# All layers' rotary tables made in the first part, scores handed over by PSUM bank, and two VectorE pieces of the feed-forward moved

## The reference, cut to what matters

```python
xn = layernorm(x)                              # x: 2 x 1024 x 128
x = x + causal_attention(xn) + stack(xn)       # both read xn

# causal_attention: 16 heads of width 8, full 1024 x 1024 scores, softmax, then a
# scrambled transpose and @ W_O

# stack: 6 layers of
x = attn_layer(shift_tokens(x), ...) + x       # 16 heads of 64, windows of 32 + the one before
x = ffn_layer(shift_tokens(x), ...) + x
# attn_layer:
q = l2norm(q) * q_scale[i];  k = l2norm(k) * k_scale[i]
q = q * cos * scale + rotate_half(q) * sin * scale
k = k * cos / scale + rotate_half(k) * sin / scale
# ffn_layer: layernorm, gain, (a, gate) = xn @ W1 + b1, a * gelu(gate) @ W2 + b2
```

## Time and profile before

| | us |
|---|---|
| runs | 2111.00, 2115.48, 2120.15 (median 2115.48) |
| profiled execution, its own time | 2128.67 |
| span of the profiled execution | 2126.9 |
| busy: PE / DVE / POOL / ACT | 1940.5 / 1658.7 / 1418.3 / 1305.8 |
| mean granted clock of TensorE | 0.953 of full |

### The profile page before, as it was taken

The page is one execution under the profiler, slowest core; times in us unless marked ns, Lnnn a source line. Parts: engine busy times, 40 slices in busy tenths (PEclk is TensorE's granted clock), DMA queues, the critical chain, the costliest instruction groups (busy, mean ns, idle before and its releaser), DMA issues.

```text
span 2126.9 us, 74573 instructions
## 1 busy us (share of the span) xinstructions
PE 1940.5 (91%) x33032; PEld 1322.8 (62%) x33032; DVE 1658.7 (78%) x1635; ACT 1305.8 (61%) x1547; POOL 1418.3 (67%) x1403
## 2 busy tenths in 40 slices
PE   3989899589999999999899998899999999999985
PEld 1434444357767666776677776667767676676774
DVE  5765562489888888889888988887888888988862
ACT  1355457356667766667666765666776666766752
POOL 1000000699988898879888888597889887888820
PEclk7799999789999999999999999999999999999997
DMA  3141100033233333333223323233333333322221
GB/s 103 39 133 46 44 25 12 28 82 77 70 86 75 87 71 77 90 78 85 63 65 87 91 71 90 49 79 86 74 86 72 79 93 74 72 63 66 69 67 45
DMA packets 144033, 151.51 MB, mean 71 GB/s; under 512 B 60760, under 2 KB 85596, under 8 KB 142944
## 3 DMA queue, kind: packets, MB, share of 16 engines
q1 hardware_dynamic: 143712, 146.75, 27.5%
HBM read 35.75 MB, written 5.44 MB: 19 GB/s over the span
## 4 chain that ended last, share of the span: by engine, by line
PE 32%; DVE 22%; POOL 21%; issue 15%; SPq 5%; ACT 3%; DMA 1%; POOLq 0%; DVEq 0%; ACTq 0%
POOL arena L1109 8%; POOL arena L1117 5%; SPq L1273 4%; DVE arena L626 4%; PE banks L408 4%; DVE ss L713 3%; PE banks L471 3%; PE banks L538 3%; PE banks L480 3%; DVE mx_t L748 3%; PE banks L565 3%; PE banks L391 2%; PE banks L498 2%; DVE arena L721 2%; PE banks L511 2%
## 5 line engine op out<-in xcount | busy, mean ns | idle before, releaser
L1109 POOL TENSOR_TENSOR arena<-arena,tab_sl 128x512 f32<-128x512 f32 x384 | 589.2, 1565 | 16.2 <-ACT arena L917 9.9
L1117 POOL TENSOR_TENSOR arena<-arena 128x1024 f32<-128x1024 f32 x192 | 488.0, 2563 | 0.0
L721 DVE TENSOR_TENSOR arena<-arena,rn 128x1024 f32<-128x1024 f32 x192 | 359.9, 1915 | 113.9 <-POOL rn L1085 113.9
L471 PE MATMUL banks<-w_qkv,arena 128*128 128x512 f32 x768 | 358.4, 609 | 8.3 <-ACT arena L909 5.5
L946 ACT ACTIVATE arena<-arena 128x1024 f32<-128x1024 f32 x96 | 101.6, 1058 | 407.9 <-DVE arena L752 407.9
L626 DVE TENSOR_REDUCE arena<-banks 128x1 f32<-128x1024 f32 (+7 forms) x176 | 175.1, 1027 | 105.1 <-PE banks L372 104.8
L538 PE MATMUL banks<-arena 64*64 64x32 f32 x12288 | 244.0, 222 | 4.0 <-DVE arena L752 3.4
L538 PEld LDWEIGHTS banks<-arena 64*64 64x64 f32 x12288 | 233.2, 135 | 16.9 <-DVE arena L752 5.3
L480 PE MATMUL banks<-ident,arena 128*128 128x128 f32 x1536 | 208.1, 291 | 33.9 <-DVE arena L762 18.5
L471 PEld LDWEIGHTS banks<-w_qkv,arena 128*128 128x128 f32 x768 | 139.4, 191 | 160.0 <-issue 150.8
L762 DVE TENSOR_TENSOR arena<-banks,tab_cl 128x1024 f32<-128x1024 f32 x192 | 226.2, 1219 | 11.8 <-ACT arena L917 10.2
(11 more groups left out here) (108 smaller groups left out, 3067.8 us busy)
## 6 DMA issues: line engine op xcount, KB each, us to landing
arena<-arena SPq DMA_DIRECT2D x1512, 64.0 KB
arena<-parts_dram SPq DMA_DIRECT2D x64, 144.0 KB
w_qkv<-Wqkv SPq DMA_DIRECT2D x6, 1024.0 KB
parts_dram<-arena SPq DMA_DIRECT2D x12, 256.0 KB, 3.1
tab_cl<-tab_c SPq DMA_DIRECT2D x6, 512.0 KB, 7.3
tab_sl<-tab_s SPq DMA_DIRECT2D x6, 512.0 KB
w_o<-Wo SPq DMA_DIRECT2D x6, 512.0 KB
w_qkv<-Wqkv SPq DMA_DIRECT2D x6, 512.0 KB, 4.6
```

Source lines behind the costliest of these rows:

```text
L471: last = e.matmul(ps[:, BANK * c:BANK * (c + 1)], xsT[b][:, P * t:P * (t + 1)], w_qkv[:, at:at + BANK], start=True, stop=True)
L721: e.tensor_tensor(to, to, rn[n // 2 % 2][:, n % 2, HEADS * m:HEADS * (m + 1)].unsqueeze(2).to_broadcast([P, HEADS, HEAD_DIM]), ALU.mult).t ...
L1109: e.tensor_tensor(qk_sw[:, m, :].rearrange("p (h d) -> p h d", d=HEAD_DIM)[:, :, d:d + HALF], raw[:, m, :].rearrange("p (h d) -> p h d", d ...
L1117: e.tensor_tensor(to, to, qk_sw[:, m, :], ALU.add).then_inc(S["rs"], 1)
```

## The change

Three edits.

1. Tables. While the causal attention runs, after the row maxima of groups 1 to 6, SP loads gains and constant tables and POOL scales them for layer 5, 4, ... 0 in turn (`make_tables`, `scale_tables`). Those of layers 5 to 2 are stored to a DRAM scratch `tabs_dram`; those of layers 1 and 0 stay in the two buffers (KEPT = 2). In the layers SP loads the finished tables of layers 2 to 5 back at step 4 of the layer before, and POOL scales nothing.
2. Scores by banks. `a_scores` and `a_weigh` signal each bank on its own and wait for the readers of that bank alone; `a_maximum` and `a_exp` become two instructions for a unit, one for each bank. Where a single head fills the pair, the first bank's maxima go to `m_first`, and one more minimum for each group joins them.
3. Feed-forward. `ff_residual` stands ahead of `subtract` in its step; `ff_stats` moves from k = 1 to k = 0, `ff_rsqrt` from k = 2 to k = 1.

```diff
+        def pieces(j, many, n, bank):
+            if many == 1:
+                return slice(j, j + 1), BANK * bank, min(n, BANK * (bank + 1))
+            return slice(j + bank * many // 2, j + (bank + 1) * many // 2), 0, n
...
-            last_on[i] = [readers[k:k + 2] for k in range(0, len(readers), 2)]
+            whole = [readers[k:k + 2] for k in range(0, len(readers), 2)]
+            first = [(done, count - 1) for done, count in whole] if by_bank else whole
+            last_on[i] = (first, whole)
...
-                place(("a_sc", k), 3, "a_max", k + 1)
+                place(("a_sc", k), 3, "a_max", 2 * k + 2, by_bank=True)
...
             def a_scores(k):
...
-                ps = pair("a_sc", k)
...
+                for bank in range(2):
+                    heads, c0, c1 = pieces(j0, many, n, bank)
+                    ps = pair("a_sc", k, bank=bank)
+                    for j in range(heads.start, heads.stop):
...
+                        last = e.matmul(ps[:, at + c0:at + c1], QS[slot][0:ROWS, P * qt:P * (qt + 1)],
+                                        KS[slot][0:ROWS, c0:c1], start=True, stop=True)
+                        if c1 == n:
+                            last = e.matmul(ps[:, at + n - P:at + n], ident_b, mask_rows, start=False, stop=True, skip_group_check=True)
+                    last.then_inc(S["a_sc"], 1)
...
             def a_maximum(k):
...
+                for bank in range(2):
+                    heads, c0, c1 = pieces(j0, many, n, bank)
+                    to = m_first[g % 2][:, qt - tiles // 2, heads] if c1 < n else m_neg[g % 2][:, qt, heads]
+                    w.wait_ge(S["a_sc"], 2 * k + bank + 1)
+                    e.tensor_reduce(to, banks[:, pair_of["a_sc", k], BANK * bank:BANK * (bank + 1)].rearrange(
+                        "p (j n) -> p j n", j=heads.stop - heads.start)[:, :, 0:c1 - c0], AX_X, ALU.max, negate=True).then_inc(S["a_max"], 1)
...
+                e.tensor_tensor(upper, upper, m_first[g % 2], ALU.min).then_inc(S["a_mstep"], 1)
...
+                if s >= FF and k == 1 and G > 0:
+                    ff_residual(G - 1)
                 if 0 <= s - 4 < n_tiles:
                     subtract(s - 4)
-                if s >= FF and k == 1 and G > 0:
-                    ff_residual(G - 1)
...
-                if ff_here and k == 1:
+                if ff_here and k == 0:
                     ff_stats(G)
...
-            scale_cos(0)
-            scale_sin(0)
+            for i, l in enumerate(reversed(range(layers))):
+                scale_tables(i, l)
...
-                if s % all_tiles == 7 and s // all_tiles + 1 < layers:
-                    scale_cos(s // all_tiles + 1)
-                if s % all_tiles == 9 and s // all_tiles + 1 < layers:
-                    scale_sin(s // all_tiles + 1)
...
-                if s >= FF and k == 2 and G < n_groups:
+                if s >= FF and k == 1 and G < n_groups:
                     ff_rsqrt(G)
...
+            def make_tables(i):
+
+                l = layers - 1 - i
+                w.wait_ge(S["tab_c"], i)
+                w.wait_ge(S["tab_s"], 2 * i)
+                if i and l + 1 >= KEPT:
+                    for m, tab in enumerate((tab_cl, tab_sl)):
+                        e.dma_start(tabs_dram[l + 1, m], tab[(l + 1) % 2][:, :, :, :]).then_inc(S["tabs_out"], 16)
...
+            def load_tables(l):
+                w.wait_ge(S["tabs_out"], 32 * (layers - KEPT))
+                w.wait_ge(S["rc"], 2 * all_tiles * (l - 1))
+                w.wait_ge(S["sw"], 4 * all_tiles * (l - 1))
+                for m, (tab, done) in enumerate(((tab_cl, "cos_in"), (tab_sl, "sin_in"))):
+                    e.dma_start(tab[l % 2][:, :, :, :], tabs_dram[l, m]).then_inc(S[done], 16)
...
+                    if 1 <= g <= layers:
+                        make_tables(g - 1)
```

More of the change, by code:

```diff
@@ L117, in build @@
     n_groups = n_tiles // GROUP
+    KEPT = 2
+    assert layers + 1 < batches * A_GROUPS
     with ExitStack() as ctx:
@@ L187, in build @@
         m_neg = [carve("A", tiles * A_PER_GROUP).rearrange("p (t j) -> p t j", j=A_PER_GROUP) for _ in range(2)]
+        m_first = [carve("A", tiles // 2 * A_PER_GROUP).rearrange("p (t j) -> p t j", j=A_PER_GROUP) for _ in range(2)]
         M_ROWS = A_PER_GROUP * PARTS * tiles
@@ L330, in tensor_program, with pair @@
             w = Once(e)
-            def pair(*use):
-                for done, count in before[use] or []:
-                    w.wait_ge(S[done], count)
+            def pair(*use, bank=1):
+                if before[use]:
+                    for done, count in before[use][bank]:
+                        w.wait_ge(S[done], count)
                 return banks[:, pair_of[use], :]
@@ L622, in a_maximum @@
                 n = P * (qt + 1)
-                w.wait_ge(S["a_sc"], k + 1)
                 if g >= 2:
                     w.wait_ge(S["a_mlo"], g - 1)
-                e.tensor_reduce(m_neg[g % 2][:, qt, j0:j0 + many],
-                                banks[:, pair_of["a_sc", k], :].rearrange("p (j n) -> p j n", j=many)[:, :, 0:n],
-                                AX_X, ALU.max, negate=True).then_inc(S["a_max"], 1)
+                for bank in range(2):
+                    heads, c0, c1 = pieces(j0, many, n, bank)
+                    to = m_first[g % 2][:, qt - tiles // 2, heads] if c1 < n else m_neg[g % 2][:, qt, heads]
+                    w.wait_ge(S["a_sc"], 2 * k + bank + 1)
+                    e.tensor_reduce(to, banks[:, pair_of["a_sc", k], BANK * bank:BANK * (bank + 1)].rearrange(
+                        "p (j n) -> p j n", j=heads.stop - heads.start)[:, :, 0:c1 - c0], AX_X, ALU.max, negate=True).then_inc(S["a_max"], 1)
             def a_maxima_split(g):
@@ L756, in rotate @@
                 l, b, t = of_tile(n)
-                w.wait_ge(S["tab_c"], l + 1)
+                w.wait_ge(S["tab_c"], layers)
+                if l >= KEPT:
+                    w.wait_ge(S["cos_in"], 16 * (layers + l - KEPT + 1))
                 w.wait_ge(S["tk"], max(0, n - 3))
@@ L865, in a_exp @@
                 n, quad = seq - P * kt, g * tiles + kt
-                w.wait_ge(S["a_wsc"], s + 1)
                 w.wait_ge(S["a_gather"], max(0, quad - 1))
-                e.activation(pt_ring[quad % 2][:, j0:j0 + many, 0:n],
-                             banks[:, pair_of["a_wsc", s], :].rearrange("p (j n) -> p j n", j=many)[:, :, 0:n], ACT.Exp,
-                             scale=float(A_DIM) ** -0.5).then_inc(S["a_exp"], 1)
+                for bank in range(2):
+                    heads, c0, c1 = pieces(j0, many, n, bank)
+                    w.wait_ge(S["a_wsc"], 2 * s + bank + 1)
+                    e.activation(pt_ring[quad % 2][:, heads, c0:c1],
+                                 banks[:, pair_of["a_wsc", s], BANK * bank:BANK * (bank + 1)].rearrange(
+                                     "p (j n) -> p j n", j=heads.stop - heads.start)[:, :, 0:c1 - c0], ACT.Exp,
+                                 scale=float(A_DIM) ** -0.5).then_inc(S["a_exp"], 1)
             def a_copy_sums(g):
@@ L1301, in sync_program @@
                     load_layer(G // (batches * halves) + 1)
-                if s % all_tiles == 4 and s // all_tiles + 1 < layers:
-                    load_gains(s // all_tiles + 1)
+                if s % all_tiles == 4 and KEPT <= s // all_tiles + 1 < layers:
                     load_tables(s // all_tiles + 1)
@@ L1341 @@
     rows_dram = nc.dram_tensor("rows_dram", [shape[0] * A_GROUPS, 3 * shape[1] * A_PER_GROUP // P, P], BF16, kind="Internal").ap()
-    build(nc, ins, out, scratch, parts_dram, rows_dram)
+    tabs_dram = nc.dram_tensor("tabs_dram", [arrays["Wqkv"].shape[0], 2, P, shape[1] // P, 2, HEAD_DIM], F32, kind="Internal").ap()
+    build(nc, ins, out, scratch, parts_dram, rows_dram, tabs_dram)
     result = run_bass_kernel_spmd(nc, [arrays], core_ids=[0])
```

83 lines of the change are left out of this document (34 added, 49 removed).

## The result

| | us | ratio to before, 95% interval |
|---|---|---|
| before, four runs beside the changed kernel | 2113.24 | |
| changed kernel, four runs (2147.73 to 2171.47) | 2157.53 | 1.0212 (1.0137 to 1.0287) |
| its profiled execution, own time | 2147.73 | span 2145.8 |

The change made the kernel slower by 2%, outside the forecast range (2060 to 2145, likeliest 2102). By their medians the tables' edit brings 9 to 17 us, the banks' edit 33, and the feed-forward edit costs 86; and that loss hangs on one copy of 127 rows. Cut into a copy of 112 and one of 15 rows, the same kernel takes 2035.5 us (ratio 0.968), the best of all. The profiled execution of the changed kernel (2147.73) is the fastest of its four, so what its trace shows of the loss is rather too little.

A forecast was written before the change was run, and what follows sets the result against it. TensorE was taken to bound plain layers, VectorE's maxima to hold 25.2% of the first part's chain; 2128.67 - 28.6 - 13 + 22 = 2109, less half the profile-to-median gap, gave 2102 us, range 2060 to 2145.

The forecast's parts named there:

- the statistics' term: Layers' feed-forward: statistics one step up wait for shifted rows, +0.5 us for each of 22 groups, +22 us together.
- R1: Rival, chance 0.17: in the layers the wait for shifted rows decides; slower, 2146 us at a landing 3 us later.
- Landing: Shifted-row copy in the layers: rows land 1.55 us after the copy's issue ends, as measured on a window copy.
- Scaling: Layers, VectorE behind the statistics: the scaling by norms takes 3.28 us, ahead of residual and maxima.
- R3: Rival, chance 0.13: in the layers the statistics fall into VectorE's idle and nothing behind them slips; 2045 us.
- Banks: First part, causal attention: splitting scores by banks removes TensorE's waits for VectorE; -13 us together.
- The start: First part, 30 units ahead of the first weighing: each split maximum costs 0.14 us on VectorE's chain, +4.2 us.
- the periods: First part, 6.6 periods of 22 units: 2.6 of 3.5 us idle won in each, -17.2 us.
- R4: Rival, chance 0.15: banks bring nothing in the first part, since VectorE becomes the bound; 2115, up to 2140 us.
- Tables: Layers 1 to 4: moving GpSimd's table scalings into the first part removes them and the waits they cause; -28.6 us.
- R2: Rival, chance 0.13: the layers' long VectorE multiplications are not the tables' and stay or move; 2131 us.
- Half of the 13.2 us between profile and median: Whole kernel: half the profiled execution's excess over the runs' median taken off, 2109 to 2102 us.

The follow-up runs named there:

- e1: Changed kernel with the whole feed-forward edit undone, leaving tables and banks; 2070.99 us, ratio 0.9814 to before.
- e9: Changed kernel with the shifted-row copy of 127 rows cut into 112 and 15 rows; 2035.53 us, ratio 0.968 to before.
- e3: Kernel before with scores handed over by banks alone; 2079.94 us, ratio 0.9858 to before.
- e5: Tables and banks edits plus the residual ahead of the maxima, statistics in their old place; 2065.34 us, ratio 0.9803 to before.
- e10: e5 with the copy of 127 rows cut into 112 and 15 rows; 2066.53 us, ratio 0.9827 to before.

## Why the prediction was wrong, by its own steps

**The step that failed is the statistics' term: +22, measured +86.** The wait was named (VectorE waits for the shifted rows, and R1 made that the losing case). What follows from it was priced wrong, or left out, in four places:

- Landing: 1.55 us taken from a window copy, 2.02 to 2.17 in all 24 groups of after. By my own rate of 22 us for each us that is 11 us. The Trainium skill's fixed cost of about 2.0 us (DMA: Bandwidth & Descriptors, Anatomy of one DMA, which is written for copies that GpSimd issues) was nearer than my row.
- Scaling: 3.28 taken, but an instruction that starts later starts inside GpSimd's rotation. The first scaling behind the statistics took 4.0 us or more in 16 of 22 groups. The scalings of steps 1 and 2 together take 9.9 us a group, against 8.0 in e1 and 7.4 in e9 (same order of instructions, rows in time). The same line of the page, after and then e9:

```profile
L741 DVE TENSOR_TENSOR arena<-arena,rn 128x1024 f32<-128x1024 f32 x192 | 407.5, 2162 | 46.2 <-POOL rn L1106 46.2
```

```profile
L741 DVE TENSOR_TENSOR arena<-arena,rn 128x1024 f32<-128x1024 f32 x192 | 352.2, 1875 | 96.0 <-POOL rn L1106 96.0
```

- TensorE: I followed the chain DVE, ACT, shifted projection, and left out that the output projection waits for the residual, which starts at P1 + 5.6 in group 18 before, and now at P1 + 6.3 there and at P1 + 8.8 in group 2. TensorE's wait for it went from 8.1 to 49.1 us.
- Clock: behind these gaps TensorE ran slow. Six groups keep 1.00 in step k = 1; their steps 1 and 2 last 33.2 us in the mean (199.0/6). Fifteen others had 0.72 to 0.92 there and last 34.8 (522.5/15). Without the edit (e1) it is 31.7. So 6 x 1.5 + 15 x 3.1 + 10.5 for group 0 = 66 us, out of 69 by which all four steps grew. In k = 1 the growth is 66 us of idle and 38 of slower matmuls, as shown above; the sum had no term for the second.

R1's own price had a slip: at the 22 us that the sum gives to each us of later landing, 3 us later is 2168 us and not 2146. By that rate the measured time would need a landing 2.5 us later; it was 0.5. So a later landing doesn't account for the loss; most of it is what the wait set off.

Behind these lies the deeper omission: I took the end of the copy's issue as given and asked how much later the rows land, not why an issue of 768 bytes holds SyncE for 7 us. With that question R3's mechanism is right: with rows in time the edit gains 31 us, near the 35 that R3 put on it.

**Banks: -13, measured -33** (-28.5 in the trace of after). The start was put at +4.2 and cost +1.5, made good by the 45th unit. In the periods I bounded the gain by the visible idle, 3.5 us of 39, and took 2.6; a period gave 6.0, of which about 3 us came at an equal clock and about 3 with a higher one. The row had it: 0.91 stands in the earlier trace rows. R4 is refuted by e3.

**Tables: -28.6, measured -9 to -17.** The layers' excess was read from one execution that held three long multiplications, 28.0 us together. R2 (they are not the tables') is refuted as to cause but right as to worth: mostly they don't occur. Half of the 13.2 us between profile and median I had taken off for this; the tables' term itself was what needed it.

**Sum.** -17 - 33 + 86 = +36 on 2113 gives 2149, and the run gave 2157.5; the parts add up within the few us that each of them is uncertain by. Of the signs I set out: steps 1 and 2 at 34.7 us in the mean (R1's was over 35, mine 32 to 33), no multiplication of line 741's kind above 3 us, VectorE's waits before the statistics of 4.5 to 7.3 us in 21 of 24 groups (forecast 4 to 6), 11.8 in group 0, a period shorter by 6.0 (forecast 2 to 3). The chance of slower was 0.27.

## What to carry to other kernels

When an edit puts a wait on a copy, look at the issue *behind* the copy and at the DMA share while it lasts: a share of a sixteenth means one engine, and a row count that 16 divides, with the rest apart, can turn the edit's sign (2157.5 to 2035.5 us here, against 2113 before). Price a late instruction with what it meets at its new time and with the clock of what waits for it, not by its old duration alone. And read a term from more than one execution when a few rare long instructions carry it.

## What the runs showed that I had not expected

- A shift by one row is a copy of 127 rows; it kept about one of 16 DMA engines busy and held the issue behind it for 7 us. As 112 + 15 rows the issue behind takes 0.75 us. Made a step earlier instead, 34 us were lost in the steps k = 0.
- With the banks' edit most periods of the first part ran at a granted clock of 1.00 that ran at 0.91 before, and about half of a period's gain came with it. It isn't certain: in e5 one was at 0.87.
- A multiplication of VectorE with both inputs in SBUF, begun a little after GpSimd's, ended 1.1 us behind the last of six GpSimd instructions (8.97 us for 1.2).
- In the best kernel steps k = 3 are 17 us longer in sum than in e10 (449.8 against 432.8): nearly every second one takes 21 us or more, where e10's take 19.8. What takes this back is open.
